# Contiguous queries for the row maxima, and the table of maxima turned on VectorE before it is copied

## The chip, the cores and the metric

The kernel runs on one core of a Trainium2 chip. The metric is the device time of one launch in microseconds. A core has TensorE (PE, with its weight loads shown as PEld), VectorE (DVE), ScalarE (ACT), GpSimd (POOL) and SyncE (SP), which only issues DMAs here. All engines run their own instruction streams in order and meet at semaphores.

## The reference

x is 8 x 768 x 32 x 32 (B = 8 images, C = 768 channels, N = 1024 pixels). It is normalised in 32 groups, sent through attention with 12 heads of 64 channels, and added to itself:

```
q = Wq @ gn(x); k = Wk @ gn(x); v = Wv @ gn(x)
scores = q^T k / sqrt(64)            # per image and head: 1024 x 1024
attn = softmax(scores over the keys)
out = x + Wp @ (attn applied to v)
```

## The kernel before

`project_phase` computes q, k and v for all images and writes them to DRAM in two parts, high and low. The change leaves it alone. `attend_phase` walks over 48 pairs of heads (two heads lie on partitions 0 to 63 and 64 to 127). A pair p has eight steps t, one for each 128 keys. In each step PE makes the scores by key (`scores_by_key`, L751: for both halves of the queries four products on each head: three of q and k, and one of `ones_r` with the row `top`, which subtracts each query's maximum), ACT takes the exponential (L877), PE multiplies with v (`values`, L764), and POOL adds the exponentials up (L707).

The maxima come one pair ahead. While pair p runs, PE makes the scores of pair p + 1 once more, with the queries on the partitions, in 16 units of two matmuls (`scores_by_query`, L734). `UNITS_BY_STEP` places them: three in step 0 (one at its very start, one after `values` of the pair before and the output group, one after the scores by key), then two in each of steps 1 to 6 (one after the scores by key and before `values`, one after `values`), one in step 7. DVE reduces each unit to the negated maximum of its 512 keys (`unit_max`, L924). After the last unit DVE joins the two halves of the keys (`join`, L930) into `neg_max`, 128 partitions x 2 heads x 8. SP then copies the table to one row per head, `top`, on partitions 0 and 64 (`maxima`, L564: two DMAs, 128 pieces of 32 bytes each). PE waits for `top` (L740) before the first score by key of the pair. Since the row must be in the order of the queries and a partition writes eight neighbours of it, unit t reads the queries t, t + 8, t + 16 and so on: the weights of L734 are read with a stride of 8 elements (L733).

From pair 7 on PE also makes two output groups in each pair (`output`, L783: 18 matmuls with a piece of wp and of `a`, the attention's result, which comes back from DRAM): `group(0)` in step 0, between `values` of the pair before and the second unit, and `group(1)` in step 4. The six tiles of `a` are loaded anew in every third pair. Four of them are issued ahead of `maxima`, and two behind it.

The order of SP's DMAs in a pair (`pair` in `@block.sync`) is: q and k of pair p + 2 (L553, L554); store and load of one y (L594, L598); v (L558); the sums of the pair before (L573) and their reciprocals (L579, L582); the other y; the four loads of `a` (L606) where they are due; `maxima(p + 1)`, which waits for the join; both parts of the result of the pair before (`store_head`, L612, L614); and the last two loads of `a`, of which the first waits until that store has landed (L605). DVE also has the reciprocals (L934) in step 3 and the additions of x (L940).

Of the kernel before, what the change touches and what calls it, by code (L numbers as in the profile page):

```python
# [6 lines left out]
F32R = mybir.dt.float32r  # L7
I32 = mybir.dt.int32
ALU = mybir.AluOpType
ACT = mybir.ActivationFunctionType  # L10
AX = mybir.AxisListType

P = 128
# [6 lines left out]
def f32(ap):  # L20

    return ap.bitcast(F32)
# [380 lines left out]
def attend_phase(nc, S, x, wp_rows, q_dram, k_dram, v_dram, o_dram, recip_dram, out, psum):  # L403
    B, C, N, KT, DH, MT = S.B, S.C, S.N, S.KT, S.DH, S.MT
    NP = B * KT
    SLOTS = 3
# [11 lines left out]
    QUARTER = P // 4  # L418
    SUMS_AT, SUM_COPY_AT, RECIP_AT, DIVIDE_AT, HIGH_AT, LOW_AT = 1, 2, 3, 4, 5, 5
    ADDS = 2 * (MT - 1)  # L420
    GROUPS_OF = 2 * KT
    assert sum(map(sum, UNITS_BY_STEP)) == UNITS and MT == 8 and 2 * DH == P
    assert BODY % SLOTS == 0 and BODY % V_SLOTS == 0 and (BODY * MT) % EXPS == 0
# [6 lines left out]
    with ExitStack() as ctx:  # L430
        def sb(name, shape, dt=F32):
            return ctx.enter_context(nc.sbuf_tensor(name, shape, dt))

        def sem(name):
            return ctx.enter_context(nc.semaphore(name))

        q = sb("q", [P, SLOTS, 2, N], F32R)
        k = sb("k", [P, SLOTS, 2, N], F32R)
        top = sb("top", [P, SLOTS, N], F32R)
# [3 lines left out]
        p_all = sb("p_all", [P, 2, EXPS, N])  # L443
        sums = sb("sums", [P, 2, 2, N])
        half_max = sb("half_max", [P, 2, MT, 2])
        neg_max = sb("neg_max", [P, 2, 2, MT], F32R)
        total = sb("total", [P, BANK])
        compact = sb("compact", [P, 2, MT])
        recip_all = sb("recip_all", [P, N])
# [4 lines left out]
        a = sb("a", [P, KT, 2, BANK], F32R)  # L454
# [15 lines left out]
        set_done = sem("set_done")  # L470
        top_in = sem("top_in")
        rows_ready = sem("rows_ready")
        max_done = sem("max_done")
        neg_done = sem("neg_done")
        s_ready = sem("s_ready")
        exp_done = sem("exp_done")
# [27 lines left out]
        def wait(eng, s, n):  # L504

            if not (known(n) and n <= 0):
                eng.wait_ge(s, n)
# [33 lines left out]
        TAIL = 2 * (NP - LAG)  # L541
        LAST = [(half, ot) for half in range(2) for ot in range(KT)]
        LAST_BANKS = (1, 2, 3, 4, 5, 6, 0, 7, 1, 2, 3, 4)
        SETS = 3
        block = ctx.enter_context(nc.Block())

        @block.sync
        def _(sp):
# [11 lines left out]
            def maxima(p, m):  # L560

                sp.wait_ge(neg_done, p + 1)
                for i in range(2):
                    sp.dma_start(f32(top[i * DH:i * DH + 1, m % SLOTS, :]).rearrange("a (p t) -> a p t", t=MT),  # L564
                                 f32(neg_max[:, m % 2, i, :])).then_inc(top_in, 16)

            def gather_totals(p):

# [104 lines left out]
            sp.wait_ge(pv_done, NP * MT)  # L673
            sp.wait_ge(added, NP * ADDS)
            sp.dma_start(y_last, x[B - 1].rearrange("(o p) (h n) -> p o h n", p=P, h=2)).then_inc(x_last_in, 16)
# [10 lines left out]
        def _(pool):  # L686
# [10 lines left out]
            def pair(p, m, u):  # L697
                for t in range(1, MT):
                    for i in range(2):
# [4 lines left out]
                        if t > 1:  # L704
                            pool.wait_ge(added, p * ADDS + 2 * (t - 2) + i + 1)
                        first = p_all[:, i, (n - 1) % EXPS, :] if t == 1 else sums[:, m % 2, i, :]
# [15 lines left out]
        def _(pe):  # L722
# [3 lines left out]
            def scores_by_query(p, m, u, unit, to=rows, taken=None):  # L726
                t, h = unit // 2, unit % 2
                e = m % SLOTS
                if unit == 0:
                    pe.wait_ge(qk_in[e], 32 * (turn(p, m, u) + 1))  # L730
                wait(pe, max_done, p * UNITS + unit if taken is None else taken)
                for i, part in enumerate(half_of):
                    queries = q[part, e, 0, :].rearrange("p (n t) -> p t n", t=MT)[:, t, :]  # L733
                    mm = pe.matmul(to[:, i, :], queries, k[part, e, 0, h * BANK:(h + 1) * BANK], start=True, stop=True)  # L734
                mm.then_inc(rows_ready, 1)

            def scores_by_key(p, m, t, h):
                e = m % SLOTS
                if t == 0 and h == 0:
                    pe.wait_ge(top_in, 32 * (p + 1))  # L740
                wait(pe, exp_done, (p * MT + t) * 4 + 2 * h - 2)
                if h == 1 and t in (OUT_AT[0], OUT_AT[1] + 1) and at_least(p, LAG):
                    pe.wait_ge(y_done, (p - LAG) * 2 + (1 if t == OUT_AT[0] else 2))
                if h == 1 and t == SUMS_AT + 1:
                    wait(pe, sum_copied, p)
                cols, keys = slice(h * BANK, (h + 1) * BANK), slice(t * P, (t + 1) * P)
                for c in range(4):
                    for i, part in enumerate(half_of):
                        left, right = ((k[part, e, 0, keys], q[part, e, 0, cols]), (k[part, e, 0, keys], q[part, e, 1, cols]),
                                       (k[part, e, 1, keys], q[part, e, 0, cols]), (ones_r[part, :], top[part, e, cols]))[c]  # L750
                        mm = pe.matmul(psum[:, SCORE_BANKS[2 * h + i], :], left, right, start=(c == 0), stop=(c == 3))  # L751
                        if c == 3:
                            mm.then_inc(s_ready, 1)
# [14 lines left out]
            def add_up(p, m):  # L768

                pe.wait_ge(added, (p + 1) * ADDS)  # L770
                for i in range(2):
# [15 lines left out]
            for unit in range(UNITS):  # L787
                scores_by_query(0, 0, None, unit, to=heads if unit % 2 else rows, taken=unit - 1)
            pe.wait_ge(set_done, SETS)

# [76 lines left out]
        def _(act):  # L867
            def exponent(p, m, t, h):
                n = p * MT + t
                for i in range(2):  # L870
                    if h == 0:
                        back = t - EXPS
                        if i == 0:
                            wait(act, pv_done, n - EXPS + 1)
                        wait(act, added, p * ADDS + (2 * max(back, 1) if back >= 0 else 2 * back + 2) - 1 + i)
                    act.wait_ge(s_ready, n * 4 + 2 * h + i + 1)
# [40 lines left out]
        @block.vector  # L917
        def _(dve):
            def unit_max(p, m, unit, of=rows):
                t, h = unit // 2, unit % 2  # L920
                dve.wait_ge(rows_ready, p * UNITS + unit + 1)
                if unit == 0:
                    wait(dve, neg_done, p)
                dve.tensor_reduce(half_max[:, :, t, h], of, AX.X, ALU.max, negate=True).then_inc(max_done, 1)  # L924

            def join(p, m):

                dve.wait_ge(max_done, (p + 1) * UNITS)
                wait(dve, top_in, 32 * (p - 1))
                dve.tensor_reduce(neg_max[:, m % 2, :, :], half_max[:], AX.X, ALU.min).then_inc(neg_done, 1)  # L930

            def reciprocals(p):
                dve.wait_ge(compact_in, 64 * (p + 1))
                dve.reciprocal(compact[:], compact[:]).then_inc(recip_done, 1)  # L934

            def add_x(n, s, count, bank=small):

                dve.wait_ge(kt_done, (n + 1) * KT)
                dve.wait_ge(x_in[s], 16 * count)
                dve.tensor_tensor(y[:, s, :], bank, y[:, s, :], ALU.add).then_inc(y_done, 1)  # L940

            dve.memset(ones[:], 1.0).then_inc(set_done, 1)
            dve.memset(f32(ones_r[:]), 1.0).then_inc(set_done, 1)
            dve.memset(f32(top[:]), 0.0).then_inc(set_done, 1)
            for unit in range(UNITS):
                unit_max(0, 0, unit, heads if unit % 2 else rows)
            join(0, 0)

            def pair(p, m, u):
                first, last = known(p) and p == 0, known(p) and p == NP - 1  # L950
                for t in range(MT):
                    front, behind, late, end = units(t) if not last else [()] * 4
                    for unit in front:
                        unit_max(p + 1, m + 1, unit)
                    if t == OUT_AT[0] and at_least(p, LAG):
                        add_x((p - LAG) * 2, 0, p - LAG + 1)
                    for unit in (*behind, *late):
                        unit_max(p + 1, m + 1, unit)
                    if t == MT - 1 and not last:
                        join(p + 1, m + 1)  # L960
                    if t == OUT_AT[1] and at_least(p, LAG):
                        add_x((p - LAG) * 2 + 1, 1, p - LAG + 1)
                    if t == RECIP_AT and not first:
                        reciprocals(p - 1)
                    for unit in end:
                        unit_max(p + 1, m + 1, unit)

            all_pairs(dve, pair)
            add_x(TAIL, 0, NP - LAG + 1)
            add_x(TAIL + 1, 1, NP - LAG + 1, psum[:, 0, :])  # L970
            reciprocals(NP - 1)
            dve.wait_ge(x_last_in, 16)
            for n, (half, ot) in enumerate(LAST):
                dve.wait_ge(last_done, n + 1)
                dve.tensor_tensor(y_last[:, ot, half, :], psum[:, LAST_BANKS[n], :], y_last[:, ot, half, :], ALU.add).then_inc(y_last_done, 1)
# [36 lines left out]
```

## Time and profile before

| | us |
|---|---|
| median of 3 runs | 3598.19 (3596.39 to 3599.04) |
| the profiled execution | 3599.69 |
| its span | 3597.9 |
| PE busy | 3451.4 |
| POOL busy | 1846.7 |
| DVE busy | 1429.2 |
| ACT busy | 1116.7 |

The span goes from the first to the last instruction. The first 1239 us of it are `project_phase`. Busy times of PE come from matmuls whose ends are modelled, and matmuls on different halves of the array overlap. So the time from one start to the next says more than a duration.

### The profile page before, as it was taken

How to read it: one execution, taken by the hardware profiler on the slowest of the kernel's cores; microseconds unless marked ns; L12 is line 12 of the kernel's file. 1: busy time of each engine (PE TensorE's matmuls, PEld its weight loads, DVE VectorE, ACT ScalarE, POOL GpSimd, SP SyncE). 2: the span in 40 equal slices, each digit the busy share in tenths (PEclk: the TensorE clock that was granted, in tenths of full speed). 3: DMA queues.
4: the chain of work that ended last, by engine and by line, in shares of the span. 5: the costliest groups of instructions: out<-in, count | busy, mean ns of one | idle time of the engine just before them, and what ended most of it. 6: DMA issues, size and time to landing. Idle time of an engine off the chain costs nothing.

```text
span 3597.9 us, 51581 instructions
## 1 busy us (share of the span) xinstructions
PE 3451.4 (96%) x18656; PEld 2374.1 (66%) x18656; DVE 1429.2 (40%) x1739; ACT 1116.7 (31%) x1992; POOL 1846.7 (51%) x795
## 2 busy tenths in 40 slices
PE   6999999999999899999999999999999999999999
PEld 5888888888888655555555555555555555555556
DVE  5333323333232255544444444444444444444431
ACT  3111111111111044533433434334343343433431
POOL 3000000000000089977878768778777777877873
PEclk9999999999999899999999999999999999999999
DMA  6233342333422423334343343443343434334324
GB/s 214 103 132 111 141 145 102 131 111 141 144 102 101 163 85 116 127 127 141 118 145 128 106 152 119 140 146 108 124 142 127 144 119 130 130 118 153 115 92 170
DMA packets 259123, 464.45 MB, mean 129 GB/s; under 512 B 60640, under 2 KB 109920, under 8 KB 257632
## 3 DMA queue, kind: packets, MB, share of 16 engines
q1 hardware_dynamic: 258912, 461.67, 37.3%
q8 instruction: 129, 2.11, 0.3%
q14 instruction: 82, 0.67, 0.1%
HBM read 260.11 MB, written 200.67 MB: 128 GB/s over the span
## 4 chain that ended last, share of the span: by engine, by line
PE 58%; DMA 4%; issue 1%; DVE 1%; SPq 1%; ACT 0%; POOL 0%; DVEq 0%; ACTq 0%; POOLq 0%
PE psum L751 20%; PE psum L764 18%; PE psum L783 9%; PE psum L734 8%; DMA a<-o_parts 2%; PE psum L845 1%; DMA o_parts<-o_lo 1%; PE psum L774 1%; DVE half_max L924 1%; SPq L564 0%; DMA q<-o_parts 0%; ACT p_all L877 0%; SPq L612 0%; DMA k<-k_parts 0%; POOL sums L707 0%
## 5 line engine op out<-in xcount | busy, mean ns | idle before, releaser
L707 POOL TENSOR_TENSOR sums<-sums,p_all 128x1024 f32<-128x1024 f32 x576 | 1352.8, 2384 | 95.3 <-ACT p_all L877 95.1
L924 DVE TENSOR_REDUCE half_max<-psum 128x2 f32<-128x1024 f32 x768 | 939.5, 1225 | 753.5 <-PE psum L734 728.1
L877 ACT ACTIVATE p_all<-psum 128x512 f32<-128x512 f32 x1536 | 793.6, 602 | 1076.8 <-PE psum L751 1074.0
L764 PE MATMUL psum<-p_all,v 128*64 128x512 f32 x3072 | 744.1, 605 | 0.0
L751 PE MATMUL psum<-q,k 64*128 64x512 f32 x4608 | 674.4, 397 | 2.0 <-ACT p_all L877 0.3
L715 POOL TENSOR_TENSOR wp<-sums,wp 128x1536 fp32r<-128x1536 f32 x1 | 3.5, 3466 | 1177.8 <-ACT wp L910 1177.8
L751 PEld LDWEIGHTS psum<-q,k 64*128 64x128 f32 x4608 | 440.2, 190 | 110.3 <-ACT p_all L877 29.8
L783 PE MATMUL psum<-a,wp 128*128 128x512 f32 x1512 | 393.3, 414 | 74.2 <-DMA a<-o_parts 74.2
L734 PEld LDWEIGHTS psum<-k,q 64*128 64x128 f32 x1536 | 243.2, 312 | 319.6 <-DVE half_max L924 199.0
L240 PE MATMUL psum<-xn_hi,w_hi 128*128 128x512 f32 x1128 | 440.8, 391 | 6.9 <-DVE stage L377 6.9
L240 PE MATMUL psum<-xn_hi,w_lo 128*128 128x512 f32 x1128 | 440.0, 390 | 0.0
L240 PE MATMUL psum<-xn_lo,w_hi 128*128 128x512 f32 x1128 | 440.0, 390 | 0.0
L734 PE MATMUL psum<-k,q 64*128 64x512 f32 x1536 | 405.7, 522 | 23.8 <-DMA k<-k_parts 10.7
L783 PEld LDWEIGHTS psum<-a,wp 128*128 128x128 f32 x1512 | 286.0, 196 | 211.2 <-DMA a<-o_parts 86.0
L707 POOL TENSOR_TENSOR sums<-p_all 128x1024 f32<-128x1024 f32 x96 | 226.8, 2385 | 374.5 <-ACT p_all L877 374.5
L290 ACT CAST stage<-psum 128x512 fp32r<-128x512 f32 x192 | 112.6, 588 | 969.1 <-PE psum L240 963.6
L764 PEld LDWEIGHTS psum<-p_all,v 128*64 128x64 f32 x3072 | 186.4, 136 | 314.8 <-issue 308.1
L377 DVE TENSOR_TENSOR stage<-psum,stage 128x512 fp32r<-128x512 f32 x192 | 132.4, 691 | 542.6 <-ACT stage L290 542.4
L751 PE MATMUL psum<-top,ones_r 64*128 64x512 f32 x1536 | 306.6, 393 | 0.0
L940 DVE TENSOR_TENSOR y<-psum,y 128x512 f32<-128x512 f32 x84 | 58.1, 691 | 523.6 <-PE psum L783 523.6
L240 PE MATMUL psum<-w_hi,xn_hi 128*128 128x384 f32 x768 | 257.3, 335 | 0.0
L240 PE MATMUL psum<-w_hi,xn_lo 128*128 128x384 f32 x768 | 256.7, 334 | 0.0
(72 smaller groups left out, 2500.7 us busy)
## 6 DMA issues: line engine op xcount, KB each, us to landing
q_parts<-stage SPq DMA_DIRECT2D x192, 256.0 KB, 2.2
k_parts<-stage SPq DMA_DIRECT2D x192, 256.0 KB, 2.3
q<-q_parts SPq DMA_DIRECT2D x48, 1024.0 KB, 6.7
k<-k_parts SPq DMA_DIRECT2D x48, 1024.0 KB, 8.8
a<-o_parts SPq DMA_DIRECT2D x84, 512.0 KB, 6.1
v_rows<-stage SPq DMA_DIRECT2D x128, 192.0 KB, 2.1
v<-v_rows SPq DMA_DIRECT2D x48, 512.0 KB, 3.9
recip_all<-recip_rows SPq DMA_DIRECT2D x96, 256.0 KB, 3.9
```

Of the source, the lines that this page charges most:

```text
L240: mm = pe.matmul(out, lhs, rhs, start=(kt == 0 and n == 0), stop=(kt == KT - 1 and n == 2))
L290: act.copy(stage[:, r, 0:BANK], psum[:, r, :]).then_inc(hi_done, 1)
L377: dve.tensor_tensor(stage[:, r, BANK:2 * BANK], psum[:, r, :], f32(stage[:, r, 0:BANK]), ALU.subtract).then_inc(lo_done, 1)
L707: pool.tensor_tensor(sums[:, m % 2, i, :], first, p_all[:, i, n, :], ALU.add).then_inc(added, 1)
L734: mm = pe.matmul(to[:, i, :], queries, k[part, e, 0, h * BANK:(h + 1) * BANK], start=True, stop=True)
L751: mm = pe.matmul(psum[:, SCORE_BANKS[2 * h + i], :], left, right, start=(c == 0), stop=(c == 3))
L764: mm = pe.matmul(heads[part, h, :], v[:, e, t, part], p_all[:, i, (m * MT + t) % EXPS, cols], start=(t == 0), stop=(t == MT - 1))
L774: mm = pe.matmul(totals[c * QUARTER:(c + 1) * QUARTER, :], ones[:], sums[:, m % 2, i, cols], start=True, stop=True)
L783: mm = pe.matmul(bank, wp[:, wpart, kt, ot * P:(ot + 1) * P], a_of[kt][:, apart, :], start=first, stop=final)
L877: act.activation(p_all[:, i, (m * MT + t) % EXPS, h * BANK:(h + 1) * BANK], psum[:, SCORE_BANKS[2 * h + i], :], ACT.Exp, scale=SCALE).then ...
L924: dve.tensor_reduce(half_max[:, :, t, h], of, AX.X, ALU.max, negate=True).then_inc(max_done, 1)
L940: dve.tensor_tensor(y[:, s, :], bank, y[:, s, :], ALU.add).then_inc(y_done, 1)
```

## The change

- L733: unit t reads 128 neighbouring queries, so the weights are contiguous. Row j of the table now stands for query 128 t + j.
- `join` becomes three dependent DVE instructions: the reduction into `neg_max` (now 128 x 32 with columns 16 to 31 zero), a transpose of its 32 x 32 blocks into `flipped`, and a copy of that to `turned`, which is of type float32r and has two slots. Each waits for the one before it on a new semaphore `joined`.
- `maxima` issues eight DMAs in place of two: for each head four, one for each block of 32 partitions. Each moves 8 partitions x 32 elements to eight stretches of 128 bytes of the row.
- PE and DVE wait for 128 on `top_in` in place of 32 for each pair. DVE clears `neg_max` once at the start.

```diff
-        neg_max = sb("neg_max", [P, 2, 2, MT], F32R)
+        neg_max = sb("neg_max", [P, SQUARE])
+        flipped = sb("flipped", [P, SQUARE])
+        turned = sb("turned", [P, 2, SQUARE], F32R)
...
                 sp.wait_ge(neg_done, p + 1)
                 for i in range(2):
-                    sp.dma_start(f32(top[i * DH:i * DH + 1, m % SLOTS, :]).rearrange("a (p t) -> a p t", t=MT),
-                                 f32(neg_max[:, m % 2, i, :])).then_inc(top_in, 16)
+                    for b in range(P // SQUARE):
+                        rows_of = slice(b * SQUARE + i * MT, b * SQUARE + (i + 1) * MT)
+                        sp.dma_start(f32(top[i * DH:i * DH + 1, m % SLOTS, :]).rearrange("a (t b j) -> a b t j", t=MT, j=SQUARE)[:, b, :, :],
+                                     f32(turned[rows_of, m % 2, :])).then_inc(top_in, 16)
...
-                    queries = q[part, e, 0, :].rearrange("p (n t) -> p t n", t=MT)[:, t, :]
+                    queries = q[part, e, 0, t * P:(t + 1) * P]
...
-                dve.tensor_reduce(neg_max[:, m % 2, :, :], half_max[:], AX.X, ALU.min).then_inc(neg_done, 1)
+                dve.tensor_reduce(neg_max[:, 0:2 * MT].rearrange("p (i t) -> p i t", i=2), half_max[:], AX.X, ALU.min).then_inc(joined, 1)
+                dve.wait_ge(joined, 2 * p + 1)
+                dve.transpose(flipped[:], neg_max[:]).then_inc(joined, 1)
+                dve.wait_ge(joined, 2 * p + 2)
+                dve.tensor_copy(turned[:, m % 2, :], flipped[:]).then_inc(neg_done, 1)
```

## Rows read from the trace of the kernel before

**Rows 1.** The page: busy us of each engine (share of the span) and instructions.
```profile
PE 3451.4 (96%) x18656; PEld 2374.1 (66%) x18656; DVE 1429.2 (40%) x1739; ACT 1116.7 (31%) x1992; POOL 1846.7 (51%) x795
```

**Rows 2.** Timeline, start us, us, engine line operation xcount: join to pair 2.
```profile
1341.76 0.19 DVE L930 TENSOR_REDUCE neg_max<-half_max 128x16 fp32r<-128x32 f32 x1
...
1341.98 1.17 SPq L564 DMA_DIRECT2D top<-neg_max  x2
...
1345.15 0.62 PE L751 MATMUL psum<-q,k 64*128 64x512 f32 x4
```

**Rows 3.** Issues of the table: count, KB each, median us from issue to landing.
```profile
top<-neg_max SPq DMA_DIRECT2D x96, 4.0 KB, 2.0
```

**Rows 4.** The same for pair 25, with loads of a behind the maxima.
```profile
2409.09 0.19 DVE L930 TENSOR_REDUCE neg_max<-half_max 128x16 fp32r<-128x32 f32 x1
2409.31 1.18 SPq L564 DMA_DIRECT2D top<-neg_max  x2
...
2414.94 1.06 SPq L606 DMA_DIRECT2D a<-o_parts  x2
...
2419.88 2.98 PE L783 MATMUL psum<-a,wp 128*128 128x512 f32 x6 [4.95 <-DMA a<-o_parts]
```

**Rows 5.** The same for pair 26, with an output group, without loads of a.
```profile
2462.57 0.18 DVE L930 TENSOR_REDUCE neg_max<-half_max 128x16 fp32r<-128x32 f32 x1
...
2470.16 0.39 PE L751 MATMUL psum<-q,k 64*128 64x512 f32 x2
```

**Rows 6.** The page's groups: operation, shapes, count | busy us, mean ns | idle, releaser.
```profile
L751 PEld LDWEIGHTS psum<-q,k 64*128 64x128 f32 x4608 | 440.2, 190 | 110.3 <-ACT p_all L877 29.8
...
L734 PEld LDWEIGHTS psum<-k,q 64*128 64x128 f32 x1536 | 243.2, 312 | 319.6 <-DVE half_max L924 199.0
```

**Rows 7.** Timeline, PE, one step and the start of the next.
```profile
2436.07 0.63 PE L734 MATMUL psum<-k,q 64*128 64x512 f32 x2
...
2436.53 0.86 PE L751 MATMUL psum<-q,k 64*128 64x512 f32 x6
...
2438.36 0.42 PE L734 MATMUL psum<-k,q 64*128 64x512 f32 x2
...
2438.72 1.94 PE L764 MATMUL psum<-p_all,v 128*64 128x512 f32 x8
...
2440.58 0.62 PE L734 MATMUL psum<-k,q 64*128 64x512 f32 x2
```

**Rows 8.** Timeline, PE, the last pair, which has no units of L734.
```profile
3503.03 0.39 PE L751 MATMUL psum<-top,ones_r 64*128 64x512 f32 x2
3503.36 1.94 PE L764 MATMUL psum<-p_all,v 128*64 128x512 f32 x8
```

**Rows 9.** By line: a DVE instruction of one element, 32 of them.
```profile
L348 DVE TENSOR_SCALAR t<-t x32: 153/154/156, 17.3 to 1022.4; 128x1 f32<-128x1 f32 x32
```

**Rows 10.** Timeline, DVE and POOL, start of the projection.
```profile
28.29 2.05 DVE L357 CAST xn_hi<-xn 128x512 fp32r<-128x512 f32 x1
30.38 2.18 DVE L359 TENSOR_TENSOR xn_lo<-xn,xn_hi 128x512 fp32r<-128x512 f32 x1
32.48 0.41 DVE L357 CAST xn_hi<-xn 128x512 fp32r<-128x512 f32 x1
...
19.88 10.18 POOL L305 TENSOR_TENSOR w_lo<-stage,w_hi 128x768 fp32r<-128x768 f32 x5 [19.42 <-DVE shift L350]
```

**Rows 11.** Timeline, POOL, around the join at 2409.09.
```profile
2406.28 9.38 POOL L707 TENSOR_TENSOR sums<-sums,p_all 128x1024 f32<-128x1024 f32 x4
```

**Rows 12.** Timeline, SP, pair 26: the issues ahead of and at the sums.
```profile
2476.34 0.33 SPq L558 DMA_DIRECT2D v<-v_rows  x1
2478.46 2.48 SPq L573 DMA_DIRECT2D compact<-total  x4
```

**Rows 13.** Stores of the projection, by line: duration ns min/median/max, first and last start.
```profile
L175 SPq DMA_DIRECT2D q_parts<-stage x192: 332/332/849, 42.9 to 1188.3; - x192
```

**Rows 14.** Window: us, busy of PE, PEld, DVE, ACT, POOL, then the granted clock.
```profile
2419.80:2423.40 3.60, 3.52 (x8) 2.19 (x10) 0.41 (x1) 0.00 (x0) 0.00 (x0) 0.50 1.02 414
```

More of the change, by code:

```diff
@@ L420, in attend_phase @@
     ADDS = 2 * (MT - 1)
+    SQUARE = 32
+    TOPS = 16 * 2 * (P // SQUARE)
     GROUPS_OF = 2 * KT
@@ L473, in attend_phase @@
         max_done = sem("max_done")
+        joined = sem("joined")
         neg_done = sem("neg_done")
@@ L543, in attend_phase @@
         LAST_BANKS = (1, 2, 3, 4, 5, 6, 0, 7, 1, 2, 3, 4)
-        SETS = 3
+        SETS = 4
         block = ctx.enter_context(nc.Block())
@@ L739, in scores_by_key @@
                 if t == 0 and h == 0:
-                    pe.wait_ge(top_in, 32 * (p + 1))
+                    pe.wait_ge(top_in, TOPS * (p + 1))
                 wait(pe, exp_done, (p * MT + t) * 4 + 2 * h - 2)
@@ L928, in join @@
                 dve.wait_ge(max_done, (p + 1) * UNITS)
-                wait(dve, top_in, 32 * (p - 1))
-                dve.tensor_reduce(neg_max[:, m % 2, :, :], half_max[:], AX.X, ALU.min).then_inc(neg_done, 1)
+                wait(dve, top_in, TOPS * (p - 1))
+                dve.tensor_reduce(neg_max[:, 0:2 * MT].rearrange("p (i t) -> p i t", i=2), half_max[:], AX.X, ALU.min).then_inc(joined, 1)
[3 more added lines that the diff above has]
+                dve.tensor_copy(turned[:, m % 2, :], flipped[:]).then_inc(neg_done, 1)
             def reciprocals(p):
@@ L944, in _ @@
             dve.memset(f32(top[:]), 0.0).then_inc(set_done, 1)
+            dve.memset(neg_max[:], 0.0).then_inc(set_done, 1)
+            dve.wait_ge(set_done, SETS)
             for unit in range(UNITS):
```

## The prediction

> **What bounds the kernel.** I read the page's busy shares first, then the groups, then timelines of single pairs. PE is busy 96% of the span, POOL 51%, DVE 40% [rows 1]. So an engine other than PE matters only where PE waits for it or for a DMA that it releases. Two places of a pair decide. One is the stream of matmuls between two joins. The other is the stretch from a join to the first score by key of the next pair, where the table must go through SP and a DMA into `top`.
>
> In that stretch the pairs are of three kinds. **Pairs 1 to 6** have no output group. For pair 2 the join starts at 1341.76; the two DMAs take SP 1.17 us from 1341.98, and PE starts the pair at 1345.15 [rows 2]. The later DMA is issued about 0.6 before SP's end, at 1342.55, and lands 2.0 later [rows 3], at 1344.55. So 0.6 us are spare. **The 14 pairs 7, 10, ... 46** load `a` behind the maxima: join 2409.09, table issued until 2410.49, then the stores of the head, then `a` at 2414.94, and PE, which has stood for 4.95 us, goes on at 2419.88 [rows 4]. Every microsecond that SP loses between join and `a` is lost by PE. **The other 27** have a group: join 2462.57, landing by the same count at 2465.35, PE needs it at 2470.16 [rows 5]: 4.8 us are spare.
>
> **What the change gives: the weights of L734.** A load of L734 takes 312 ns, one of L751, same shape but contiguous, 190 [rows 6]; the stride is the only difference in form, so I take off 0.12 us. What of it lies on the path depends on what runs beside it. After `values` the load is exposed: from the unit's start to that of L751 it is 0.46 us [rows 7], about twice what a pair of matmuls takes within L751 (0.86 us for three pairs with their tail [rows 7]), so I count the whole 0.12 us for each unit that follows `values` or a group. Six such units lie between two joins, two behind the join. The seven units between scores and `values` have their load under the matmul before. From unit to L764 it is 0.36 us there [rows 7], and without a unit 0.33 from L751 to L764 [rows 8]: 0.03 at most, I take 0.02 each. The unit of step 0 after the scores is followed by a wait for ACT; nothing. So between two joins 6 x 0.12 + 7 x 0.02 = 0.86 us, and 2 x 0.12 = 0.24 behind the join: 1.10 us a pair, 52 us for 47 pairs if nothing else came.
>
> **What it costs: the way of the table.** Call D the delay of whatever stands behind the maxima on SP, against the join.
>
> - On DVE the reduction stays (0.19 us). Two waits are added, under 0.04 each (the cast that ends at 30.34 is followed at 30.38 by the instruction that waits for it [rows 10]), the transpose and the copy. The transpose has no row. A one-element instruction takes 0.154 us [rows 9] and the join's reduction, which reads 32 elements, 0.19 [rows 2]; I take 0.19, and no less than 0.15. A gain is excluded, since it is added work in a dependent chain.
> - The copy is float32 to float32r, SBUF to SBUF, as is L357. That one takes 0.41 us alone, but 2.05 when POOL runs beside it: it starts at 28.29, while POOL's five instructions from 19.88 last until 30.06, and ends at 30.34, just behind that POOL instruction [rows 10]. So it waits for POOL's current instruction to end. At the joins POOL adds without a break: four from 2406.28 in 9.38 us, one every 2.34 [rows 11]. Today's join would put the copy at 2409.54, and the instruction then running ends near 2411.0, 1.5 later. Making the join 0.86 us earlier in the pair moves the copy to within 0.1 us of a boundary: it waits either 0.1 or 2.3 us, and my terms can't say which. I take the middle, 1.2, and keep both ends. With 0.05 for the copy's own end this part is 0.07 + 0.19 + 1.2 + 0.05 = 1.5 us (0.4 to 2.65).
> - A rule of the Trainium skill bears on this (SBUF — State Buffer, Who interferes with whom): a copy that runs in a two-port mode and a GpSimd instruction exclude each other for a whole instruction, while a reduction does not take part. The trace agrees for the cast (2.05 against 0.41 us). Without that exclusion the sum below would be 40 us in place of 83.
> - SP issues six DMAs more. Small DMAs in a row take it 2.48 us for four [rows 12], 0.62 each; the cheapest plain store takes 0.33 [rows 13], 0.37 with the gap. I take 0.62, since those four are the nearest form (pieces of 32 bytes, one side on a single partition): 3.7 us (2.2 to 3.8). The landing after the last issue I leave as it is, 2.0 us.
>
> D = 1.5 + 3.7 = **5.2 us** (2.6 to 6.5).
>
> **Where D falls.**
>
> - Pair 0: PE has nothing else to do before it, and its units follow each other at DVE's pace, so there is no gain to set against D. +5.2 us.
> - Six pairs 1 to 6: D - 0.6 - 0.86 = +3.7. PE then stands over 5 us in each, as it does today in the pairs with loads, and behind such a stand the granted clock is 0.50, the lower level of 1.2 GHz, in the stretch 2419.8 to 2423.4 [rows 14]. I add 1.5 us for that (0 to 2.5). 6 x 5.2 = +31.
> - Fourteen pairs with loads: D - 0.86 - 0.12 (one unit lies behind the stand) = +4.2; +59.
> - 27 others: the need is 5.2 against 4.8 spare, +0.4, less 0.86: -0.46; -12.
>
> Behind the maxima SP also has, in ordinary pairs, q, k, y and v. Today v is issued at 2476.34 and the sums at 2478.46 [rows 12], when ACT has them: 1.8 us spare. D makes these late by some 3 us. The sums are wanted by DVE in step 3, three steps of 4.51 us [rows 7] behind 2470.16 and more: near 2486. They would land at about 2478.5 + 3 + 1.9 + 1.8 = 2485.2. That is covered, barely; beyond D = 6 DVE would wait there and PE for its units.
>
> Sum: 5.2 + 31 + 59 - 12 = **+83 us**. The profiled execution took 3599.7 (span 3597.9 and 1.8 around it), 1.5 above the median. So 3683, or 3682 against the runs' median. With D = 4.0 (copy at a boundary) it is +40, with D = 6.3 +136.
>
> **The rivals.**
>
> - *Cheap issue, slower or same.* SP issues the small pieces at the plain store's price, 0.37, and the copy meets a boundary: D = 2.6, and the sum is 2.5 + 7 + 22 - 30 = +2; with the copy held 1.2 it is +25. 3600 to 3635. Against it: both rows of small pieces are dearer.
> - *Faster.* The six DMAs cost SP next to nothing and the copy isn't held: D = 0.4. Pair 0 +0.4; pairs 1 to 6 nothing, since POOL's 16 instructions of 2.34 us already need 37.5 us in each; 14 x (0.4 - 1.0) = -8; 27 x -1.10 = -30: 3562. It decides below D = 2.5, where 21 D = 52. [...] Against it stand 1.17 us for two DMAs of the table.
> - *Transpose held as well as copy.* Each waits for POOL, and the second for a whole instruction. D = 7.5, and and 7.5 + 6 x 7.5 + 14 x 6.5 + 27 x 1.8 = +193: near 3792. Nothing in the trace shows a transpose.
> - *The weights don't get faster.* Then all of the cost comes without the gain of 52: near 3735. Against it: the stride is all that differs.
>
> **Chances.** The forecast with D between 4.0 and 6.3 (3640 to 3735) 0.66. Cheap issue 0.12, a third of it within 0.2% of no change. Faster 0.08. Both held 0.07. No gain 0.03. Something else 0.04. The range goes from 3605 to 3745 and leaves out the faster case, both held and a bit of the others. About 0.2%, 7 us, is what a measurement can tell from no change. Faster 0.08, same 0.05, slower 0.87.
>
> **What would show it.** LDWEIGHTS of L734 at 184 ns. Eight issues of the table in about 5 us. A copy of up to 2.4 us that ends with a POOL instruction. PE waiting for `top` in pairs 0 to 6 (now hardly) and for `a` about 9 to 10 us in place of 5. The half clock also in the first pairs. The prediction fails if the eight issues take under 2.5 us, or if POOL gives way to the copy.

## The result and the profile after

| | before, us | after, us |
|---|---|---|
| median of the runs compared | 3597.29 (3596.22 to 3599.04) | 3728.14 (3722.33 to 3738.5) |
| the profiled execution | 3599.69 | 3738.5 |
| its span | 3597.9 | 3736.7 |
| PE busy | 3451.4 | 3424.0 |
| DVE busy | 1429.2 | 1529.6 |
| mean granted clock of TensorE | 0.981 | 0.964 |

The changed kernel is slower, at a ratio of 1.0366 (1.0343 to 1.039), or +131 us between the medians. The profiled execution is the slowest of its four, 139 us above the one of before. The account by pairs below is taken from it, so it sums to 139 and not to 131.

The page of after: part 1, the chain by engine and by line, and the group of the weights.

```profile
PE 3424.0 (92%) x18656; PEld 2290.4 (61%) x18656; DVE 1529.6 (41%) x1836; ACT 1117.8 (30%) x1992; POOL 1847.9 (49%) x795
...
PE 45%; SPq 7%; DMA 7%; DVE 5%; issue 2%; POOL 0%; ACT 0%; DVEq 0%; ACTq 0%; POOLq 0%
PE psum L758 18%; PE psum L771 13%; SPq L571 6%; PE psum L790 6%; PE psum L741 6%; DVE turned L941 2%; DVE half_max L931 2%; DMA a<-o_parts 2%; DMA out<-y 1%; PE psum L852 1%; DMA o_parts<-o_lo 1%; DMA top<-turned 1%; PE psum L781 1%; DMA compact<-total 0%; DMA q<-o_parts 0%
...
L741 PEld LDWEIGHTS psum<-k,q 64*128 64x128 f32 x1536 | 148.6, 189 | 343.7 <-DVE half_max L931 221.7
```

PE has fallen from 96% to 92%. The issue of the table by SP (L571) and the new copy (`turned`, L941) hold 6% and 2% of the chain that ended last: no work of PE covers them. The weights did get cheaper, from a mean of 312 ns [rows 6] to 189.

The same kernel by line: duration ns as min/median/max, first and last start, shapes.

```profile
L939 DVE STREAM_TRANSPOSE flipped<-neg_max x48: 211/211/214, 1265.9 to 3622.1; 128x32 f32<-128x32 f32 x48
L941 DVE CAST turned<-flipped x48: 385/1760/9634, 1266.1 to 3622.4; 128x32 fp32r<-128x32 f32 x48
L571 SPq DMA_DIRECT2D top<-turned x384: 620/629/1536, 1268.0 to 3629.1; - x192
```

The transpose takes 0.21 us in all 48 pairs. The copy takes anything from 0.39 to 9.6 us. All 48 copies end 0.035 to 0.044 us behind the end of a POOL instruction, the shortest too, so none of them ran free and its own duration can't be read here.

Now an ordinary pair, the answer to [rows 5] and [rows 11]: timeline around the join ahead of pair 23 (start us, us, engine, line, operation, count).

```profile
2397.05 9.42 POOL L714 TENSOR_TENSOR sums<-sums,p_all 128x1024 f32<-128x1024 f32 x4
...
2399.58 0.19 DVE L937 TENSOR_REDUCE neg_max<-half_max 128x16 f32<-128x32 f32 x1
2399.80 0.21 DVE L939 STREAM_TRANSPOSE flipped<-neg_max 128x32 f32<-128x32 f32 x1
...
2400.05 1.76 DVE L941 CAST turned<-flipped 128x32 fp32r<-128x32 f32 x1
...
2401.83 5.45 SPq L571 DMA_DIRECT2D top<-turned  x8
...
2408.44 0.73 PE L758 MATMUL psum<-q,k 64*128 64x512 f32 x4 [1.36 <-DMA top<-turned]
```

From the join's start to the first issue it is now 2.25 us (2399.58 to 2401.83), where it was 0.22 [rows 4]. One of POOL's four instructions of 2.36 us ends at 2399.41 and the next at 2401.76. The copy starts 0.64 into the second of them and ends at 2401.81, just behind it. The eight issues stand 0.69 apart (5.45 us less one issue of 0.63, over seven gaps), so the last one comes 7.07 us behind the join (2.25 + 4.82), where it was 0.8. **That is D = 6.3 us**: 2.0 on DVE and 4.3 on SP. PE has its first score 8.86 us behind the join, where it was 7.59 [rows 5], and stands 1.36 us for it. It starts 1.8 us after the last issue, so the landing is a little shorter than the 2.0 that I counted.

The load pair that answers to [rows 4], as a timeline, and behind it two windows on the same stretch (us, busy of PE, PEld, DVE, ACT, POOL, the granted clock, DMA share, GB/s).

```profile
2494.46 0.19 DVE L937 TENSOR_REDUCE neg_max<-half_max 128x16 f32<-128x32 f32 x1
...
2494.92 1.75 DVE L941 CAST turned<-flipped 128x32 fp32r<-128x32 f32 x1
...
2496.70 5.53 SPq L571 DMA_DIRECT2D top<-turned  x8
...
2506.64 1.06 SPq L613 DMA_DIRECT2D a<-o_parts  x2
...
2511.62 2.96 PE L790 MATMUL psum<-a,wp 128*128 128x512 f32 x6 [11.44 <-DMA a<-o_parts]
```

```profile
2506.40:2512.50 6.10, 0.88 (x2) 0.79 (x3) 0.00 (x0) 0.00 (x0) 0.00 (x0) 0.50 0.71 209
2512.50:2515.10 2.60, 2.60 (x8) 1.38 (x8) 0.39 (x1) 0.00 (x0) 0.00 (x0) 0.50 1.02 416
```

From join to the loads of `a` it is 12.18 us, where it was 5.85 [rows 4]: the same D of 6.3, read a second way. From those loads to PE's return it is as before (4.98 and 4.94). PE stands 11.44 us in place of 4.95, and comes back at the half clock, 1.2 GHz, as it did before [rows 14].

An early pair, the answer to [rows 2].

```profile
1355.88 0.19 DVE L937 TENSOR_REDUCE neg_max<-half_max 128x16 f32<-128x32 f32 x1
...
1356.35 0.39 DVE L941 CAST turned<-flipped 128x32 fp32r<-128x32 f32 x1
1356.77 5.48 SPq L571 DMA_DIRECT2D top<-turned  x8
...
1363.33 0.80 PE L758 MATMUL psum<-q,k 64*128 64x512 f32 x2 [4.16 <-DMA top<-turned]
```

Here the copy was held only shortly: it started 0.34 us before the running POOL instruction ended and took that boundary. The last issue comes 5.7 us behind the join (0.89 + 4.85), D is 4.9, and PE stood 4.16 us for `top`. Its granted clock behind that stand, in the window:

```profile
1363.00:1370.00 7.00, 6.66 (x40) 4.63 (x42) 1.70 (x2) 3.96 (x8) 2.94 (x2) 0.76 0.97 351
```

0.76 is a mean of both levels. In windows of 2 us from 1363 on the clock reads 0.52, 0.62, 1.00 and 1.00: some 3.4 us ran at 1.2 GHz. In another early pair the copy was held as long as POOL had work. Timeline of DVE, of POOL and of PE, pair 4:

```profile
1440.96 0.18 DVE L937 TENSOR_REDUCE neg_max<-half_max 128x16 f32<-128x32 f32 x1
...
1441.43 9.63 DVE L941 CAST turned<-flipped 128x32 fp32r<-128x32 f32 x1
...
1439.43 2.39 POOL L702 TENSOR_TENSOR o_lo<-o,o_hi 128x1024 fp32r<-128x1024 f32 x1
1441.74 9.28 POOL L714 TENSOR_TENSOR sums<-sums,p_all 128x1024 f32<-128x1024 f32 x4
1464.93 2.36 POOL L714 TENSOR_TENSOR sums<-p_all 128x1024 f32<-128x1024 f32 x1 [13.90 <-ACT p_all L884]
...
1452.45 0.80 PE L741 MATMUL psum<-k,q 64*128 64x512 f32 x2 [8.62 <-DVE half_max L931]
```

The copy ends at 1451.06, 0.04 behind the fourth of POOL's additions (1451.02). So it lost to five POOL instructions in turn, one running and four more, and it ended when POOL had no more work: the next addition starts 13.9 us later. The hold costs PE on a second way. The reduction of the unit before (`half_max`) stands behind the copy on DVE and starts only at 1451.17. PE, whose next unit needs that reduction done, stands 8.62 us for it, before it waits for `top` at all. In pair 1 (5.24 us of hold) it stands 4.23 us so.

To see the whole, I took the first score by key of each pair from the trace and added up the distances from one to the next, by kind of pair. A pair's distance is the one that ends at its first score. The right-hand column goes to the end of the span.

| kernel | to pair 0 | pairs 1 to 6 | 14 with loads (each of them) | 27 others (each) | rest |
|---|---|---|---|---|---|
| before | 1268.8 | 226.9 | 739.7 (52.84) | 1258.5 (46.61) | 104.0 |
| after | 1274.7 | 268.8 | 818.1 (58.43) | 1269.2 (47.01) | 106.0 |
| difference | +5.9 | +41.9 | +78.4 | +10.7 | +2.0 |

### The profile page after: what moved, and what is told of

It reads as the page before. It is cut to its first block, busy times and chain, and to the rows that moved or that the text cites. A ratio compares the mean times of both kernels' runs of the same rounds, so it can differ in the third digit from the quotient of the medians.

```text
span 3736.7 us, 52027 instructions
## 1 busy us (share of the span) xinstructions
PE 3424.0 (92%) x18656; PEld 2290.4 (61%) x18656; DVE 1529.6 (41%) x1836; ACT 1117.8 (30%) x1992; POOL 1847.9 (49%) x795
## 4 chain that ended last, share of the span: by engine, by line
PE 45%; SPq 7%; DMA 7%; DVE 5%; issue 2%; POOL 0%; ACT 0%; DVEq 0%; ACTq 0%; POOLq 0%
PE psum L758 18%; PE psum L771 13%; SPq L571 6%; PE psum L790 6%; PE psum L741 6%; DVE turned L941 2%; DVE half_max L931 2%; DMA a<-o_parts 2%; DMA out<-y 1%; PE psum L852 1%; DMA o_parts<-o_lo 1%; DMA top<-turned 1%; PE psum L781 1%; DMA compact<-total 0%; DMA q<-o_parts 0%
## 5 line engine op out<-in xcount | busy, mean ns | idle before, releaser
L758 PE MATMUL psum<-q,k 64*128 64x512 f32 x4608 | 688.7, 404 | 66.2 <-DMA top<-turned 64.2
L741 PE MATMUL psum<-k,q 64*128 64x512 f32 x1536 | 357.2, 460 | 42.4 <-DVE half_max L931 26.7
L741 PEld LDWEIGHTS psum<-k,q 64*128 64x128 f32 x1536 | 148.6, 189 | 343.7 <-DVE half_max L931 221.7
```

## The experiments

The theory was the forecast's: contiguous weights give some 50 us, six more DMAs cost some 85, the held copy the rest, and together they push SP's queue, where the loads of `a` wait behind the table. The rivals: the copy is harmless, or the number of DMAs is, or the weights give nothing.

**The weights alone.** The kernel before with one line changed. It leaves out the turning, so the row holds the maxima in another order.

```diff
-                    queries = q[part, e, 0, :].rearrange("p (n t) -> p t n", t=MT)[:, t, :]
+                    queries = q[part, e, 0, t * P:(t + 1) * P]
```

> The kernel before with only L733 changed: a unit reads 128 neighbouring queries; join and the two DMAs stay. The row then holds the maxima in another order, so each query has another query's maximum subtracted; the work is the same. Theory (weights are the whole gain and lie on PE's path where they follow values or a group): LDWEIGHTS of L734 at 184 ns, 0.7 to 0.86 us less between joins, 1.1 us a pair less, 45 to 52 us faster: about 3548. Rival (PE waits for something else in their place, POOL in the early pairs or a in the pairs with loads): under 25 us faster.

Measured: 3552.31, ratio 0.9873 (0.9857 to 0.9889), -45 us. Its page, and a line of its waits (who, for what: us in total, times, longest).

```profile
L734 PEld LDWEIGHTS psum<-k,q 64*128 64x128 f32 x1536 | 147.2, 188 | 324.7 <-DVE half_max L924 202.8
```

```profile
ACT p_all L877 <- POOL sums L707: 39.4, 17, 2.4
```

In the 13 ordinary pairs that follow another ordinary one, the stretch from the first score to the next join falls from 38.48 to 37.63 us, and in the median of all 27 the one from join to first score from 7.60 to 7.35: 0.85 and 0.25 where 0.86 and 0.24 were counted. In the 14 that follow a load pair the first stretch falls by 0.6 on average. Over all 27 the mean gain is 1.03 us, and 0.84 in a load pair (0.98 counted). The pairs 1 to 6 gain 0.6 each (37.2 after 37.8). POOL has 16 instructions of 2.34 us, 37.4 us, in each of them. It has no idle time at all from pair 3 to pair 6, and ACT waits for it: POOL sets their length.

**The way of the table alone.** The changed kernel with that line put back (it leaves out what puts the row into the order of the queries).

```diff
-                    queries = q[part, e, 0, t * P:(t + 1) * P]
+                    queries = q[part, e, 0, :].rearrange("p (n t) -> p t n", t=MT)[:, t, :]
```

> The changed kernel with the strided queries back (old L733): transpose, copy and eight DMAs alone. The row then holds the maxima in another order. Theory (cost of the table's way and gain of the weights add up): the change's +131 plus the 45 to 52 us of the weights, 3775 to 3785. Rival (the two overlap, since both sit on the same waits): no more than 3750.

Measured: 3780.28, ratio 1.0507 (1.0468 to 1.0545), 52 above after, with runs from 3767 to 3796. The copy, by line:

```profile
L941 DVE CAST turned<-flipped x48: 1427/1444/9011, 1265.2 to 3669.3; 128x32 fp32r<-128x32 f32 x48
```

About 183 us were thus spent on the way of the table. That the difference is the 52 us forecast for the weights is in part luck, since the copies fall otherwise too. Of the 46 us between the two profiled executions 23 lie in pairs 1 to 6, where three copies were held for 8.9 us (after has one such hold). In the 27 others the difference is 0.36 us each and not 1.10, in part because the copy is 0.32 us shorter here.

**Without the copy.** The reduction rounds to float32r, and the transpose writes the table that SP reads. `flipped` and the copy are gone.

```diff
-        neg_max = sb("neg_max", [P, SQUARE])
-        flipped = sb("flipped", [P, SQUARE])
+        neg_max = sb("neg_max", [P, SQUARE], F32R)
...
-                dve.wait_ge(joined, 2 * p + 1)
-                dve.transpose(flipped[:], neg_max[:]).then_inc(joined, 1)
-                dve.wait_ge(joined, 2 * p + 2)
-                dve.tensor_copy(turned[:, m % 2, :], flipped[:]).then_inc(neg_done, 1)
+                dve.wait_ge(joined, p + 1)
+                dve.transpose(f32(turned[:, m % 2, :]), f32(neg_max[:])).then_inc(neg_done, 1)
```

> The changed kernel without the copy on VectorE: the reduction rounds to float32r itself and the transpose writes turned. Theory (the copy waits for the GpSimd instruction that runs, 1.75 us in ordinary pairs and up to 9.6 in two of the first): first issue 0.5 us behind the join in place of 2.25, no wait for top in ordinary pairs (27 x 1.3), 14 x 1.75 less before a, and the two long holds gone: 65 to 80 us faster than the changed kernel, about 3655. Rival (the time goes to the eight DMAs themselves and the copy is hidden): 3715 or more. If the transpose is held by GpSimd as well, it is near 3725.

Measured: 3642.71, ratio 1.0126 (1.0109 to 1.0142), 85 us less than after (65 to 80 expected). By line, and the timeline of pair 2:

```profile
L938 DVE STREAM_TRANSPOSE turned<-neg_max x48: 211/211/213, 1264.3 to 3530.7; 128x32 f32<-128x32 f32 x48
...
1346.91 0.19 DVE L936 TENSOR_REDUCE neg_max<-half_max 128x16 fp32r<-128x32 f32 x1
1347.13 0.21 DVE L938 STREAM_TRANSPOSE turned<-neg_max 128x32 f32<-128x32 f32 x1
1347.37 5.48 SPq L570 DMA_DIRECT2D top<-turned  x8
```

From join to first issue it is 0.46 us, 1.8 less than after, and the transpose is never held, though POOL adds beside it. The account by pairs shows why 1.8 us turn into 85: the load pairs take 56.23 us in place of 58.43, the others 45.50 in place of 47.01, and the pairs 1 to 6 18.4 us less together. The 45.50 are what the weights alone gave (45.58), so without the copy the 27 others have their full gain, and after has none of it.

**Eight DMAs alone.** The kernel before with its own table, sent in eight pieces.

```diff
-                    sp.dma_start(f32(top[i * DH:i * DH + 1, m % SLOTS, :]).rearrange("a (p t) -> a p t", t=MT),
-                                 f32(neg_max[:, m % 2, i, :])).then_inc(top_in, 16)
+                    for b in range(4):
+                        rows_of = slice(b * QUARTER, (b + 1) * QUARTER)
+                        sp.dma_start(f32(top[i * DH:i * DH + 1, m % SLOTS, :]).rearrange("a (p t) -> a p t", t=MT)[:, rows_of, :],
+                                     f32(neg_max[rows_of, m % 2, i, :])).then_inc(top_in, 16)
...
-                    pe.wait_ge(top_in, 32 * (p + 1))
+                    pe.wait_ge(top_in, 128 * (p + 1))
```

> The kernel before with its table sent in eight pieces in place of two (each 32 partitions, 32-byte pieces as before); nothing else. Theory (SP's issue time is what costs, 0.69 us each): last issue 4.8 us behind the first in place of 0.6, 4.2 us x 14 pairs with loads, 4.2 less 0.6 in the six first and 1 us each for the lower clock, nothing in the others (4.8 spare): +85 to +95, near 3687. Rival (DMAs are cheap to issue; what costs in the changed kernel is the form of its pieces or DVE's part): under +20.

Measured: 3679.57, ratio 1.0231 (1.0214 to 1.0248), +82 us, a little under the range expected. The timeline of pair 25:

```profile
2457.62 0.19 DVE L932 TENSOR_REDUCE neg_max<-half_max 128x16 fp32r<-128x32 f32 x1
2457.83 5.01 SPq L566 DMA_DIRECT2D top<-neg_max  x8
...
2467.29 1.06 SPq L608 DMA_DIRECT2D a<-o_parts  x2
...
2472.35 2.97 PE L785 MATMUL psum<-a,wp 128*128 128x512 f32 x6 [8.89 <-DMA a<-o_parts]
```

Eight issues take 5.01 us, 0.63 each, the loads of `a` come 9.67 us behind the join in place of 5.85 (D = 3.8), and PE's stand goes from 4.95 to 8.89. The pieces of the real change move 8 partitions each in place of 32, and stand 0.69 apart. The others keep 46.49 us: there the spare time covers it all.

**The copy alone.** The kernel before with the reduction into a float32 table and a copy of it. It has neither the transpose nor more DMAs.

```diff
+        joint = sb("joint", [P, 2, MT])
...
-                dve.tensor_reduce(neg_max[:, m % 2, :, :], half_max[:], AX.X, ALU.min).then_inc(neg_done, 1)
+                dve.tensor_reduce(joint[:], half_max[:], AX.X, ALU.min).then_inc(joined, 1)
+                dve.wait_ge(joined, p + 1)
+                dve.tensor_copy(neg_max[:, m % 2, :, :], joint[:]).then_inc(neg_done, 1)
```

> The kernel before with one thing more: the join's reduction goes to a float32 tile and a copy of 16 elements on VectorE rounds it into neg_max. Queries, two DMAs and order as before. Theory (the copy is held until a GpSimd instruction ends): copies of 1.5 to 2.2 us in ordinary pairs in place of 0.17, and some of 4 to 9 us in the first pairs, where GpSimd never pauses; 14 x 2 plus 6 x 1.5 plus the long holds: +35 to +65. Rival (the hold comes from the transpose before it or is hidden): under +10.

Measured: 3674.71, ratio 1.0212 (1.0195 to 1.0229), +76 us, above the range expected. By line, one copy of the early pairs from the timeline, and a line of its waits:

```profile
L934 DVE CAST neg_max<-joint x48: 1261/1706/9177, 1268.2 to 3565.0; 128x16 fp32r<-128x16 f32 x48
...
1350.47 9.17 DVE L934 CAST neg_max<-joint 128x16 fp32r<-128x16 f32 x1
...
PE psum L736 <- DVE half_max L926: 50.7, 22, 7.8
```

Pairs 1 to 6 account for the excess: they take 281.1 us, 54 more than before, since in five of them the copy was held for 9.2 us, through four POOL instructions, until POOL had no more work. They lose it not on the table: PE waits for `top` 3.7 us in the whole kernel, but of the 50.7 us above 44 lie in these pairs, where it waits for the reduction of its own unit, which stands behind the copy on DVE. So a copy of 128 x 16 elements is, with no other edit, as dear as six DMAs.

**The copy as a reduction.** To see whether it is the third instruction or the kind of instruction that costs, the changed kernel with the copy written as a reduction over an axis of length 1.

```diff
-                dve.tensor_copy(turned[:, m % 2, :], flipped[:]).then_inc(neg_done, 1)
+                dve.tensor_reduce(turned[:, m % 2, :], flipped.rearrange("p (j a) -> p j a", a=1), AX.X, ALU.min).then_inc(neg_done, 1)
```

> The changed kernel, with the copy of flipped to turned made by a reduction over one element in place of tensor_copy: the same three dependent steps and the same eight DMAs. Theory (it is the copy's form that GpSimd holds up, as it does the projection's casts and not the reductions): about 0.2 us, never held, first issue 0.7 behind the join: 3650 to 3658, the run without copy plus 14 x 0.22 and 7 x 0.22. Rival (any SBUF to SBUF instruction as third step is held, or the chain's length counts): 3700 or more.

Measured: 3654.1, ratio 1.0155 (1.0138 to 1.0172), 74 us less than after. By line:

```profile
L941 DVE TENSOR_REDUCE turned<-flipped x48: 185/186/188, 1266.0 to 3540.6; 128x32 fp32r<-128x32 f32 x48
```

Same data, same place, same waits: 0.19 us in all 48 pairs in place of 1.76. It is the kind of instruction, not the third link in the chain.

**The order on SP.** Most of the loss lies in the load pairs, because the table stands ahead of the last two loads of `a`. In three kernels `maxima` is moved behind `store_head` and those loads, from pair 6 on:

```diff
-                if not (known(p) and p == NP - 1):
+                if not at_least(p, LAG - 1):
                     maxima(p + 1, m + 1)
...
+                if at_least(p, LAG - 1) and not (known(p) and p == NP - 1):
+                    maxima(p + 1, m + 1)
```

First the changed kernel with it:

> The changed kernel, but from pair 6 on SP issues the stores of the head and the last two loads of a ahead of the maxima instead of behind them. The first pairs keep their order. Theory (in the 14 pairs with loads D costs because a stands behind the maxima on SP): PE's stand before the second part of the group falls from 11.5 us to 0.5 to 2, the half clock behind it mostly goes, 14 x 10 = 140 us less: about 3585. The maxima are then issued at 2.5 us behind the join at the earliest and land just in time. Rival (a is late for another reason, or the table becomes late behind the loads of a): 3660 or more.

Measured: 3573.98, ratio 0.9925 (0.9905 to 0.9945). The load pairs fall from 58.43 to 46.86 us each, 162 us in all, while the early ones keep the whole loss. A line of its waits:

```profile
PE psum L760 <- DMA top<-turned: 71.4, 41, 4.6
```

The stands of 4 us and more are those of pairs 1 to 6, which keep their order. In the load pairs, with the table issued last of all, PE waits for it at most 1.24 us, and for `a` at most 2.6 where it was 9.4 to 11.5. It was thus not the table that PE had missed there but `a`, as the prediction had it.

Then the same without the copy:

> Both: no copy on VectorE (as in the run without it) and stores and loads of a ahead of the maxima from pair 6 on. Theory: 3643 less 14 x 8 us and the half clock of those stands: 3520 to 3530. Rival (table late behind a): 3570 or more.

Measured: 3512.45, ratio 0.9758 (0.9742 to 0.9774), below the 3520 to 3530 expected: a load pair falls by 9.9 us against the kernel without the copy in the old order, where 8 and part of a half-clock stretch had been counted.

Then the kernel before with the new order and nothing else, to tell what of this has to do with the change:

> The kernel before with only the order on SP changed from pair 6 on: stores of the head and last loads of a ahead of the maxima. Theory (the 5 us stand of the kernel before is the same queueing): 14 x 3.5 to 4 us and the half clock behind: 50 to 65 us faster, 3535 to 3548. Rival: the stand is the landing of the store and of a alone, which the order hardly moves: under 15 us.

Measured: 3509.38, ratio 0.9749 (0.9732 to 0.9765), -89 us where I had expected 50 to 65. The timeline of a load pair, and its window:

```profile
2373.14 1.06 SPq L606 DMA_DIRECT2D a<-o_parts  x2
2374.25 1.18 SPq L564 DMA_DIRECT2D top<-neg_max  x2
2375.69 4.73 PE L785 MATMUL psum<-a,wp 128*128 128x512 f32 x18
...
2380.81 0.85 PE L753 MATMUL psum<-q,k 64*128 64x512 f32 x6
```

```profile
2370.00:2381.00 11.00, 10.93 (x54) 6.10 (x52) 3.74 (x5) 3.08 (x5) 9.44 (x5) 1.00 0.66 227
```

The group runs through, 18 matmuls in 4.73 us, the clock stays at 1.00 (2.4 GHz), and the table, issued until 2375.43, has five microseconds before PE needs it. A load pair takes 46.64 us, as much as an ordinary one (46.54): 14 x 6.2 = 87. I had counted three and a half to four microseconds of the stand and one for the clock. In this pair the whole stand and all of the half-clock stretch went; over the 14 at most 2.4 us of the stand are left. So with the old order every microsecond put between join and `a` cost the load pairs one. With the new order the old table gives 3509, and the turned one without its copy 3512. By pairs the turned one gains 25 us in the 41 pairs from 7 on, where its contiguous weights tell, and loses 29 in pairs 0 to 6, where PE waits for the last of the eight DMAs.

**Two queues.** What then still costs is the issue of eight small DMAs in a row. This kernel is the one without the copy and with the new order. In addition half of the DMAs, those of the second head, go to ScalarE's queue at the end of its pair:

```diff
-                for i in range(2):
-                    for b in range(P // SQUARE):
...
+                pieces(sp, p, m, 0)
...
+                    act.wait_ge(neg_done, p + 2)
+                    pieces(act, p + 1, m + 1, 1)
```

> The run without copy and with stores and loads of a first, and in addition ScalarE issues the four pieces of the second head at the end of its pair (it waits for the join there), SP those of the first head. Theory (what is left of the cost is SP's 0.69 us for each of eight pieces, in pairs 0 to 6): last issue 2.6 us behind the join in place of 5.3, 7 x 2.6 = 18 us faster than that run's 3512: about 3494. Rival (both engines' issues share what makes the issue slow): 3508 or more.

Measured: 3482.31 (3476.23 to 3488.61), ratio 0.967 (0.9654 to 0.9686): the fastest of all, 3.3% below the kernel before. Pair 2:

```profile
1341.67 0.18 DVE L946 TENSOR_REDUCE neg_max<-half_max 128x16 fp32r<-128x32 f32 x1
1341.89 0.21 DVE L948 STREAM_TRANSPOSE turned<-neg_max 128x32 f32<-128x32 f32 x1
1342.13 2.97 SPq L554 DMA_DIRECT2D top<-turned  x4
1342.13 2.64 ACTq L554 DMA_DIRECT2D top<-turned  x4
...
1346.44 0.74 PE L761 MATMUL psum<-q,k 64*128 64x512 f32 x4 [1.48 <-DMA top<-turned]
```

The two queues issue side by side, each four in under 3 us, and PE stands 1.48 us. The pairs 1 to 6 take 232.3 us against 250.6 with one queue, and pair 0 starts when it did before the change (1268.8). That is 30 us between the medians where 18 were expected: the early pairs gain 3.05 us each, 2.1 of it between join and first score (2.6 counted) and 0.9 behind it. Why that second part came was not tested.

## Why the prediction was right, and where its sizes were off

Predicted 3682 (3605 to 3745), slower with 0.87; measured 3728. The sign and the mechanism hold, and the time lies within the case that was called likeliest, at its upper end. By its steps:

- **The weights.** 312 to 189 ns. The count per ordinary pair was right to 0.01 us. Alone the weights give 45 us and not 52: in pairs 1 to 6 POOL sets the pace (3.7 us in all in place of 6.6), and a few of the others gain less. Inside the change they could not be measured cleanly, because taking them out moves the copies too.
- **The transpose.** 0.21 us where 0.19 was taken; held in none of 48 pairs, nor in the 48 without the copy. That rival is out.
- **The hold of the copy.** The step named two values, near 0.1 and near 2.3, depended on a phase that it couldn't compute, and took the middle, 1.2. As a rule the copy measured 1.76, which is 1.72 of waiting and 0.04 behind POOL's end (0.05 was taken). The DVE part came to 2.0 in place of 1.5. That the middle was not further off is luck: from first score to join the changed kernel takes 37.76 us in the 13 pairs that took 38.48, 0.72 less and not 0.86, and the copy starts not at a boundary but 0.64 us behind one. Not foreseen at all: in pairs 1 and 4 the copy was held for 5.24 and 9.63 us, past one boundary after another until POOL ran out of work, and PE then waited for the units behind it on DVE. The prediction counted the copy only on the way to SP. The kernels with the copy also scatter more from run to run (11 to 30 us, against 3 to 6 for most without it, and 12 for the last one), which fits holds that fall differently each time, since only the profiled executions show them; that was not tested.
- **The issue.** 0.69 us from one to the next, not 0.62: 4.3 in place of 3.7. My nearest row moved pieces of 32 bytes, while these DMAs move stretches of 128 bytes from 8 partitions. The eight DMAs alone, with 32-byte pieces from 32 partitions, gave 0.63; which of the two differences makes 0.69 was not separated.
- **D** is thereby 6.3 in place of 5.2. I had worked out the sum for just this D as +136; the profiled execution shows +139, the medians +131.
- **Where D falls.** Pair 0: +5.9 (5.2 forecast). Pairs 1 to 6: +41.9 (31), of which the two long holds are 13: their pairs took 45.9 and 52.5 us, the other four 42.6 on average. These four lost 4.8 each, where 5.2 was forecast. Load pairs: 5.60 each (4.2), with D - 0.98 = 5.3 and the rest from a stand that is a little longer than D accounts for (11.44 less 4.95 is 6.5). The 27 others: +0.40 each (-0.46). **This step carried the largest share of the error**, 23 of the 56 us between 83 and 139; the load pairs have 20 and the pairs 1 to 6 11. At D = 5.2 the table was already 0.4 us beyond its spare time; above that point every microsecond counts in those 27 pairs too. So the missing 1.1 us cost 1.1 in all 48 pairs, some 53 us, where a reader of the 21 exposed pairs alone would expect 23.
- **The clock.** The half clock does follow the longer stands in the load pairs (0.50 in both windows), and in pair 2 it appears (0.76 in the window), where the pair before the change ran at 1.00 (1341 to 1351). The forecast for an early pair was D - 0.6 - 0.86 and 1.5 for the clock. In pair 2 D is 4.9, which gives 4.9, and the four pairs without a long hold lost 4.8. The 3.4 us at the lower level are worth 1.7 us at the higher one, an estimate. From first score to the next join pairs 1 to 6 take 0.65 us more than before (35.00 after 34.35), where 1.5 less 0.86 make 0.64. So both terms fit; neither was measured by itself. POOL, which set the length of these pairs when the weights came alone, doesn't here: it idles for 4.8 us and more in each.
- **What stands behind the maxima on SP.** The prediction said that beyond D = 6 DVE would wait for the sums and PE for its units. D went there, and so it came: from pair 7 to pair 46 DVE waits for them 15 times, up to 2.9 us (in the kernel before never in these pairs), and in four of these pairs PE stands before a unit, 0.25 to 1.38 us. The sum had no term for it; the four stands make 4 us.
- **Cheap issue** is out: from one issue to the next it is 0.63 and 0.69 us, where that rival had 0.37. Alone the six DMAs added 3.8 us to D and cost 82 us. What the 0.63 us consist of, no run here shows.
- **The weights give nothing** and **faster** are out by the first experiment and the result.

The parts add up: -45 for the weights, +82 for eight DMAs, +85 for the copy (after less the kernel without it) is +122 of the +131. The transpose's 0.24 us and the wider spacing of pieces with 8 partitions (7 x 0.06 = 0.4 us), in 21 pairs and more, would be about 14 more, an estimate; 9 are left.

What stays open: why a copy takes the first boundary in one pair and is held past five in another, at nearly the same distance from it (pair 2 0.39 us, pair 4 9.63). In the four traces of kernels with a copy there are 192 of them. 176 end with the first POOL instruction that ends after their start. The other 16, all in pairs 1 to 7, end only where POOL has run out of work and idles for 9 us or more. The traces don't show what decides between the two. Nor was it tried to send the turned table in fewer DMAs, each with more partitions.

## What to carry over

Before a step is put into a chain that a DMA queue waits for, list what stands behind it in that queue: here the table's slower way hurt PE less through the table than through two loads that had nothing to do with it, and moving those ahead gave 89 us to the old kernel and 154 to the new. List what stands behind it on its own engine too: a held copy also held the reductions that PE's next units wait for. Where VectorE works beside GpSimd, choose the form of the instruction (here a reduction or a transpose in place of a copy, with the rounding done by the reduction that is there anyway), and price small DMAs by their number, 0.6 to 0.7 us each on one queue here. And where a delay meets a spare time of about its own size, the forecast gets steeper: here every further microsecond counted in 48 pairs in place of 21. Read the spare time as carefully as the delay.

## What the runs showed of the hardware

- A DVE copy of 128 x 32 float32 elements took 0.39 us at least, 1.76 in the median and 9.63 at most beside POOL's additions, and all 48 ended 0.04 us behind a POOL instruction; the same holds for the 144 of three other kernels (0.03 to 0.04). Each took either the first end of a POOL instruction or waited until POOL had no more work. Transposes of the same table took 211 to 214 ns, and reductions with as many outputs 185 to 188 ns, in all 48 pairs of each kernel. The Trainium skill (SBUF — State Buffer, Who interferes with whom) says that a copy in a two-port mode and a GpSimd instruction exclude each other for one whole instruction and that a reduction never takes part. The trace agrees on the reduction and on the ordinary copies. The 9.63 us, with four more additions of POOL started while the copy waited, are more than one instruction.
- A DMA that moves stretches of 128 bytes from 8 partitions was issued every 0.69 us by SP, one that moves 32-byte pieces from 32 partitions every 0.63, and ScalarE's queue issued four in 2.64 us, 0.66 each, while SP issued its own four. SP's four took 2.97 us, where three gaps of 0.69 and one issue of 0.63 would make 2.70; its median issue is 0.71 us there and 0.63 alone, so beside ScalarE it was slowed a little.
- A load of 64 x 128 float32 weights with a stride of 8 elements took 312 ns in the median, a contiguous one 183 to 184.
